# The peak of gate times up from magnitudes in one VectorE pass, and signed products made by batch in the down stage

## The chip, the cores and the metric

The kernel runs on one core of a Trainium2 chip. The metric is the device time of one execution in microseconds (us). PE is TensorE (its weight loads are PEld), DVE is VectorE, ACT is ScalarE, POOL is GpSimd, and SP is the engine whose queue issues most transfers.

## What is computed

`x` is 32 sequences of 128 tokens with 256 features. Four layers are added to it in turn: a cross-attention by correlation, a product in the frequency domain, a sampled cross-attention, and a feed-forward block whose tensors are all rounded to whole multiples of a unit. The change touches only the last:

```python
def act_qdq(x):
    qmax = 2.0 ** (ACT_BITS - 1) - 1.0        # ACT_BITS = 16
    scale = jnp.maximum(jnp.max(jnp.abs(x)) / qmax, 1e-12)
    return jnp.clip(jnp.round(x / scale), -qmax - 1.0, qmax) * scale
x = act_qdq(x)
up = act_qdq(x @ lpbq_dequant(w_up).T)
gate = act_qdq(x @ lpbq_dequant(w_gate).T)
sig = fixed_qdq_u16(jax.nn.sigmoid(gate))
gate = act_qdq(gate * sig)
o = act_qdq(gate * up)
return o @ lpbq_dequant(w_down).T
```

Each `act_qdq` divides by a unit that comes from the largest magnitude of the whole tensor, so nothing can be rounded before all of the tensor has been seen. `gate` and `up` have 768 features for each of the 4096 tokens.

## The kernel before

The program is written engine by engine, each with its own list of instructions, and every order and wait (semaphores) is set by hand. The features of the feed-forward block lie over the 128 partitions in IC = 6 groups, the tokens along the free dimension. Three sizes of work occur: a quad (4 sequences, 512 tokens, 8 of them), a half (256 tokens, 128x1536 elements with the six groups, HALVES = 16 of them), and a sequence (128 tokens, 128x768 elements, B = 32).

The gated product lies in `wide` (float, all tokens). `up` doesn't fit beside it: PE makes it in the stage before, ACT copies it out (`keep_up`, L1037), DVE takes its peak (`peak_up`, L1997), and the SP queue stores it to `up_far` in device memory (L593) and brings it back quad by quad into three places `ups` (L598 and L607). `up_slot` says which place a quad uses. From the fourth quad on, a transfer waits for `up_whole`, that is until ACT has read the quad that was there.

Peak stage, by halves. ACT divides `up` by its unit and writes int16 (`whole_up`, L1081, tile `upq`), and the same for the gated values (`whole_g2`, L1087, tile `g2q`), four buffers each, so that half h waits for `o_done` of half h-4 (h-3 products done). DVE multiplies the two (`hidden_product`, L2114) and writes the float product back into `wide`, then reduces it to the largest magnitude (`peak_product`, L2119), one half behind. `make_unit(4, ...)` (L1999 to L2028) turns the 16 maxima into a unit: one reduction, a transpose on PE (`spread_peak`, L1524), a second reduction and five steps on one column. PE waits for `o_peak` of 14 halves and then has three long matmuls without use (`keep_wide`, L1584) ahead of the transpose, and three behind it; they are two instructions each.

Down stage, by sequences. `staggered(engine, B, steps)` issues, at tick t, each step for sequence t minus its lag, in the order of the list. ACT multiplies the product by the inverse unit and adds a large constant, which rounds it (`round_o`, L1102); DVE subtracts the constant (`whole_hidden`, L2133); PE multiplies by the weights, 12 instructions for a sequence (`down_product`, L1591), into one of two banks; DVE scales the result and adds it to `x_sb` (`add_y`, L2138, lag 2). The SP queue stores two sequences at a time (L611), each store behind its wait for `y_done`.

Memory is laid out by hand: names that are opened and closed at once (`scrap`, `sq`, `upq` and so on) lie over others that are not alive at the same time.

Of the kernel before, what the change touches and what calls it, by code (L numbers as in the profile page):

```python
# [18 lines left out]
F32 = mybir.dt.float32  # L19
# [178 lines left out]
def build(nc, x, ctx_in, wq, wk, wv, wo, bq, bk, bv, bo, wfr, wfi, bf, wval, bval, woff, boff,  # L198
# [7 lines left out]
    with ExitStack() as ctx:  # L206
        def sem(name):
            return ctx.enter_context(nc.semaphore(name))

        def sb(name, shape, dt=F32, scope=ctx):  # L210
            return scope.enter_context(nc.sbuf_tensor(name, shape, dt))
# [19 lines left out]
        mid = sb("mid", [128, 6, 128])  # L231
        SAME, CROSS, MA, MB, INV, MEAN = (mid[:, i, :] for i in range(6))
        xn = sb("xn", [128, 4, D])
        tr_sb = sb("tr_sb", [128, 2, DC, 128])
# [173 lines left out]
            sem("gate_whole"), sem("sig_done"), [sem(f"sig_whole_{e}") for e in ("dve", "pool")], sem("g2_done"))  # L408
        up_whole, g2_whole, o_done, o_peak = sem("up_whole"), sem("g2_whole"), sem("o_done"), sem("o_peak")
        o_round, o_whole, down_out, y_done = sem("o_round"), sem("o_whole"), sem("down_out"), sem("y_done")  # L410
# [26 lines left out]
        def gate_half(h):  # L437

            return wide[:, :, h * 256:(h + 1) * 256]
# [19 lines left out]
        def up_slot(t):  # L459

            return (1, 0, 2)[t % 3]


        def ccx_rows(g):
# [60 lines left out]
        def _(sp):  # L525
# [74 lines left out]
            for t in range(1, NQ):  # L600
                for j in range(3):
                    sp.wait_ge(up_stored[j], 16 * (NQ if t == 2 else t + 1))
                if t == 2:
                    sp.wait_ge(up_peak, UPS)
                if t >= 3:
                    sp.wait_ge(up_whole, 2 * (t - 2))
                sp.dma_start(ups[:, up_slot(t)], up_far[:, t]).then_inc(up_back[t % 3], 16)  # L607
            sp.wait_ge(x3_done, 2 * NQ)
            for i in range(B // 2):
                sp.wait_ge(y_done, (i + 1) * 2)  # L610
                sp.dma_start(outr[:, i * 2:(i + 1) * 2, :], x_sb[:, i * 2:(i + 1) * 2, :]).then_inc(stored, 16)  # L611
# [158 lines left out]
        def _(act):  # L770
# [303 lines left out]
            def whole_up(h):  # L1074

                t = h // 2
                if h % 2 == 0:
                    act.wait_ge(up_back[t % 3], 16 * (t // 3 + 1))
                if h >= 4:
                    act.wait_ge(o_done, h - 3)  # L1080
                nc.scalar.activation(upq[:, h % 4], ups[:, up_slot(t), :, h % 2 * 256:(h % 2 + 1) * 256], ACT.Copy, scale=unit[:, 2, 3:4]).then_inc(up_whole, 1)  # L1081

            def whole_g2(h):

                if h >= 4:
                    act.wait_ge(o_done, h - 3)
                nc.scalar.activation(g2q[:, h % 4], gate_half(h), ACT.Copy, scale=unit[:, 3, 3:4]).then_inc(g2_whole, 1)  # L1087

# [9 lines left out]

            def round_o(b, s):
                if late(b, 2):  # L1100
                    act.wait_ge(o_whole, b - 1)
                nc.scalar.activation(hid[:, 2 + s], wide[:, :, at_seq(b)], ACT.Identity, scale=unit[:, 4, 3:4], bias=unit[:, 7, 0:1]).then_inc(o_round, 1)  # L1102

            act.wait_ge(unit_step, 1 + 5 * 5)
            staggered(act, B, [(0, round_o)])

        @block.tensor
        def _(pe):
# [477 lines left out]
            def down_product(b, s):  # L1586
                pe.wait_ge(o_whole, b + 1)
                if late(b, 2):
                    pe.wait_ge(y_done, b - 1)
                for ic in range(IC):  # L1590
                    last = mm(bank[s][:, 0:D], hid[:, s, ic, :], wdT[:, ic, :], start=(ic == 0), stop=(ic == IC - 1))  # L1591
                last.then_inc(down_out, 1)

            pe.wait_ge(up_kept, UPS)
            pe.wait_ge(o_peak, HALVES - 2)
            keep_wide(3)
# [5 lines left out]
        def _(dve):  # L1602
# [506 lines left out]

            def hidden_product(h):  # L2110

                dve.wait_ge(up_whole, h + 1)
                dve.wait_ge(g2_whole, h + 1)
                V.tensor_tensor(gate_half(h), upq[:, h % 4], g2q[:, h % 4], ALU.mult).then_inc(o_done, 1)  # L2114

            def peak_product(h):

                dve.wait_ge(o_done, h + 1)
                V.tensor_reduce(peak[:, 4, h:h + 1], gate_half(h), AX.XY, ALU.max, apply_absolute_value=True).then_inc(o_peak, 1)  # L2119

            for h in range(HALVES + 1):
                if h < HALVES:
                    hidden_product(h)
                if h:
                    peak_product(h - 1)
            dve.wait_ge(o_peak, HALVES)
            make_unit(4, HALVES)

            def whole_hidden(b, s):
                dve.wait_ge(o_round, b + 1)  # L2130
                if late(b, 2):
                    dve.wait_ge(down_out, b - 1)
                V.tensor_scalar(hid[:, s], hid[:, 2 + s], MAGIC, None, ALU.subtract).then_inc(o_whole, 1)  # L2133

# [4 lines left out]

            staggered(dve, B, [(0, whole_hidden), (2, add_y)])  # L2140

# [20 lines left out]
```

## Time and profile before

| what | value |
|---|---|
| runs of this kernel | 866.13, 871.84, 871.96 us, median 871.84 |
| the profiled execution | 868.69 us |
| its span in the profile | 866.2 us |
| mean granted clock of PE | 0.941 of full speed |
| busy, of the span | PE 84%, DVE 74%, ACT 54%, POOL 29% |

The span runs from the first to the last instruction of the profiled execution. Times in a trace are from the span's start. A pass is shown with its own duration; on ACT and DVE the next one may start before the last has ended, so start-to-start times are a little shorter than durations.

### The profile page before, as it was taken

What the parts mean: (1) busy time and instruction counts of PE and PEld (TensorE: products, weight loads), DVE (VectorE), ACT (ScalarE), POOL (GpSimd) and SP (SyncE); (2) the same over time, 40 slices, a digit from 0 to 9 for tenths busy, and PEclk for the clock granted to TensorE, in tenths of its full rate; (3) what the DMA queues carried; (4) which work ended last, traced back from release to release, by engine and by line L of the source; (5) the groups of instructions that cost most, each with busy time, mean ns of one, the idle gap of its engine ahead of it and who ended that gap; (6) DMA issues with size and microseconds to landing.
All of it is one profiled execution on the core that took longest, in us unless ns stands there. A gap on an engine that the chain in (4) does not pass through costs nothing.

```text
span 866.2 us, 10711 instructions
## 1 busy us (share of the span) xinstructions
PE 727.4 (84%) x3599; PEld 485.6 (56%) x3599; DVE 639.0 (74%) x1184; ACT 465.5 (54%) x818; POOL 249.8 (29%) x198
## 2 busy tenths in 40 slices
PE   4999998799977788767999987999979990039998
PEld 4878886578766567523455553444434440018887
DVE  3577799966798579955999975877569997993333
ACT  2444455455334668855655512344379959934441
POOL 3000000576784112365676720000023320000000
PEclk9999999799999999889999997999999995559999
DMA  8900000050143300000000000000014339501111
GB/s 279 349 12 1 1 1 0 1 135 1 30 139 85 35 1 1 2 1 1 2 2 1 1 2 0 1 0 1 0 73 163 158 147 403 219 0 37 49 52 58
DMA packets 32122, 52.87 MB, mean 61 GB/s; under 512 B 3523, under 2 KB 27331, under 8 KB 30918
## 3 DMA queue, kind: packets, MB, share of 16 engines
q1 hardware_dynamic: 30256, 50.62, 17.7%
q10 hardware_dynamic: 1814, 1.59, 0.6%
q8 instruction: 29, 0.48, 0.2%
q14 instruction: 23, 0.19, 0.1%
HBM read 35.34 MB, written 16.84 MB: 60 GB/s over the span
## 4 chain that ended last, share of the span: by engine, by line
PE 41%; ACT 11%; DVE 8%; issue 4%; DMA 1%; POOL 0%; SPq 0%; DVEq 0%; ACTq 0%; POOLq 0%
PE pair L1544 10%; PE pair L1591 10%; PE pair L1472 4%; PE pair L1440 4%; PE pair L1455 3%; DVE wide L2085 3%; PE pair L1483 2%; ACT upq L1081 2%; ACT g2q L1087 2%; PE pair L1332 2%; PE pair L1335 2%; ACT wide L1050 1%; DVE peak L1997 1%; PE pair L1569 1%; DMA ups<-up_far 1%
## 5 line engine op out<-in xcount | busy, mean ns | idle before, releaser
L1932 DVE SCALAR_TENSOR_TENSOR hat<-pair,hat 128x1024 f32<-128x1024 f32 x64 | 78.0, 1218 | 29.5 <-ACT hat L970 18.2
L970 ACT ACTIVATE hat<-pair 128x1024 f32<-128x1024 f32 x64 | 65.5, 1024 | 60.9 <-PE pair L1440 60.9
L1569 PE MATMUL pair<-xqs,wuT 128*128 128x512 f32 x192 | 84.6, 601 | 4.7 <-ACT up_stage L1037 4.7
L1544 PE MATMUL pair<-xqs,wgT 128*128 128x512 f32 x192 | 85.4, 603 | 0.0
L1591 PE MATMUL pair<-wdT,hid 128*128 128x256 f32 x384 | 83.1, 379 | 0.4 <-DVE hid L2133 0.4
L723 POOL TENSOR_TENSOR hat<-hat 128x1024 f32<-128x1024 f32 x30 | 70.7, 2357 | 41.3 <-DVE hat L1932 41.3
L1591 PEld LDWEIGHTS pair<-wdT,hid 128*128 128x128 f32 x384 | 72.9, 190 | 11.1 <-DVE hid L2133 1.2
L1569 PEld LDWEIGHTS pair<-xqs,wuT 128*128 128x128 f32 x192 | 36.8, 194 | 51.3 <-issue 51.1
L1152 PE MATMUL pair<-wT,ft_sb 128*128 128x256 f32 x256 | 63.8, 392 | 0.0
L623 POOL TENSOR_TENSOR rstd<-lnt,half 128x8 f32<-128x8 f32 (+2 forms) x15 | 26.4, 1760 | 129.5 <-DVE lnt L1635 129.5
L1102 ACT ACTIVATE hid<-wide,unit 128x768 f32<-128x768 f32 x32 | 32.5, 1026 | 57.2 <-DVE hid L2133 43.7
L1544 PEld LDWEIGHTS pair<-xqs,wgT 128*128 128x128 f32 x192 | 36.8, 195 | 43.7 <-issue 43.7
L1018 ACT ACTIVATE wide<-pair 128x512 f32<-128x512 f32 x48 | 28.7, 597 | 57.1 <-PE pair L1544 57.1
L2133 DVE TENSOR_SCALAR hid<-hid 128x768 f32<-128x768 f32 x32 | 17.9, 560 | 51.1 <-PE pair L1591 49.6
L1606 DVE BATCH_NORM_STATS2 stats<-x_sb 128x6 f32<-128x256 f32 x128 | 50.8, 414 | 5.3 <-DMA x_sb<-in_x_dram 5.3
L1152 PEld LDWEIGHTS pair<-wT,ft_sb 128*128 128x128 f32 x256 | 46.0, 189 | 12.2 <-issue 7.3
L749 POOL CAST xqs<-xqT 128x1024 f32<-128x1024 int16 x16 | 19.2, 1198 | 116.2 <-ACT xqT L1011 77.9
L1584 PE MATMUL pair<-wdT 128*128 128x512 f32 x12 | 7.7, 794 | 52.9 <-DVE peak L2119 52.9
L796 ACT ACTIVATE qq<-pair 128x256 f32<-128x256 f32 x32 | 12.3, 383 | 65.8 <-PE pair L1155 65.8
L1650 DVE TENSOR_SCALAR xn<-x_sb,rstd,nmr 128x256 f32<-128x256 f32 x96 | 46.4, 483 | 1.4 <-PE pair L1315 1.1
L1292 PE MATMUL pair<-fold,tr_sb 128*128 128x256 f32 x128 | 35.2, 399 | 12.7 <-DVE x_sb L1785 10.3
L1725 DVE TENSOR_TENSOR ab<-qq,pair 128x512 f32<-128x512 f32 x32 | 21.9, 686 | 30.1 <-ACT qq L798 29.8
(243 smaller groups left out, 1711.8 us busy)
## 6 DMA issues: line engine op xcount, KB each, us to landing
up_far<-up_stage SPq DMA_DIRECT2D x24, 512.0 KB, 2.6
ups<-up_far SPq DMA_DIRECT2D x8, 1536.0 KB, 6.9
x_sb<-in_x_dram SPq DMA_DIRECT2D x8, 512.0 KB, 7.4
c_sb<-in_ctx_dram SPq DMA_DIRECT2D x8, 512.0 KB, 8.7
ctx<-in_ctx_dram SPq DMA_DIRECT2D x32, 128.0 KB
out_dram<-x_sb SPq DMA_DIRECT2D x16, 256.0 KB, 2.1
ctx<-in_ctx_dram SPq DMA_DIRECT2D x16, 126.0 KB
four<-in_c_four_dram SPq DMA_DIRECT2D x1, 1280.0 KB, 6.6
```

The costliest lines, as they stand in the source:

```text
L723: nc.gpsimd.tensor_tensor(ramp(4 * u + 2), ramp(4 * u), ramp(4 * u + 2), ALU.add).then_inc(summed, 1)
L970: nc.scalar.activation(ramp(n), sides_of(n)[:].rearrange("p i t -> p (i t)"), ACT.Relu).then_inc(relu_done, 1)
L1152: mm(bank[2 + s][:, i * D:(i + 1) * D], ft_sb[:, s, i * DC + c, :], wT[:, i, c, :], start=False, stop=(i == 1 and c == DC - 1))
L1292: last = mm(bank[6 + s][:, 0:D], tr_sb[:, s, c, :], fold[:, c, :], start=(c == 0), stop=(c == DC - 1))
L1440: last = mm(sides_of(n)[:, i, :], sel[half, n % NP, :], rows[half, q, c * 2 + a, :], start=True, stop=True)
L1472: last = mm(bank[5][:, b * D:(b + 1) * D], attT[:, q % 2, c, (2 * i + b) * L:(2 * i + b + 1) * L], wout_sb[:, c, :], start=False, stop=(c ...
L1544: last = mm(bank[2 + oc][:], wgT[:, c, oc * 128:(oc + 1) * 128], xqs[:, s, c, :], start=(c == 0), stop=(c == DC - 1))
L1569: last = mm(bank[2 + oc], wuT[:, c, oc * 128:(oc + 1) * 128], xqs[:, t % 2, c, :], start=(c == 0), stop=(c == DC - 1))
L1591: last = mm(bank[s][:, 0:D], hid[:, s, ic, :], wdT[:, ic, :], start=(ic == 0), stop=(ic == IC - 1))
L1606: V.bn_stats(stats[:, at(b), :].rearrange("p o s -> p (o s)"), x_sb[:, at(b), :].rearrange("p o d -> p (o d)")).then_inc(bn_done[n], 1)
L1650: V.tensor_scalar(xn[:, b % 4, :], x_sb[:, at(b), :].rearrange("p o d -> p (o d)"), rstd[:, at(b)], nmr[:, at(b)], ALU.mult, ALU.add).then ...
L1932: V.scalar_tensor_tensor(ramp(n), sides_of(n)[:].rearrange("p i t -> p (i t)"), 0.0, ramp(n), ALU.max, ALU.add).then_inc(hat_done, 1)
```

## The change

ACT makes magnitudes (Abs) for the peak stage in place of signed whole parts. DVE multiplies two of them and keeps the largest in one pass (`tensor_tensor_reduce`); the product itself goes to a tile `scrap` that nobody reads, so `wide` keeps the gated values. In the down stage the signed parts are made again for one sequence at a time: the gated part on DVE (`signed_gate`), the up part on ACT (`signed_up`), their product times the inverse unit on DVE into int16 (`whole_product`), and its float form on ACT (`widen_o`) into four buffers `hid` in place of two. For this the SP queue reads `up_far` a second time (`up_again`), into two of the three places. Two of these eight transfers stand ahead of the output stores, the others between them. `add_y` moves from lag 2 to lag 3.

```diff
--- before.py
+++ after.py
@@ -230,6 +230,9 @@
         attT_place.close()
         mid = sb("mid", [128, 6, 128])
         SAME, CROSS, MA, MB, INV, MEAN = (mid[:, i, :] for i in range(6))
+        scrap_place = ExitStack()
+        scrap = sb("scrap", [128, IC, 256], F32, scrap_place)
+        scrap_place.close()
         xn = sb("xn", [128, 4, D])
         tr_sb = sb("tr_sb", [128, 2, DC, 128])
         peak = sb("peak", [128, 5, 64])
@@ -406,7 +409,7 @@
         up_stored, up_back = [sem(f"up_stored{i}") for i in range(3)], [sem(f"up_back{i}") for i in range(3)]
         gate_whole, sig_done, sig_whole, g2_done = (
             sem("gate_whole"), sem("sig_done"), [sem(f"sig_whole_{e}") for e in ("dve", "pool")], sem("g2_done"))
-        up_whole, g2_whole, o_done, o_peak = sem("up_whole"), sem("g2_whole"), sem("o_done"), sem("o_peak")
+        up_whole, g2_whole, o_done = sem("up_whole"), sem("g2_whole"), sem("o_done")
         o_round, o_whole, down_out, y_done = sem("o_round"), sem("o_whole"), sem("down_out"), sem("y_done")
         xn3_ready, tr3_done, tr3_copied = sem("xn3_ready"), sem("tr3_done"), sem("tr3_copied")
         mm3_done, v_kept, off_kept = sem("mm3_done"), sem("v_kept"), sem("off_kept")
@@ -460,6 +463,10 @@
 
             return (1, 0, 2)[t % 3]
 
+
+        def again_slot(r):
+
+            return 2 - r % 2 * 2
 
         def ccx_rows(g):
 
@@ -605,8 +612,18 @@
                 if t >= 3:
                     sp.wait_ge(up_whole, 2 * (t - 2))
                 sp.dma_start(ups[:, up_slot(t)], up_far[:, t]).then_inc(up_back[t % 3], 16)
+
+            def up_again(r):
+
+                sp.wait_ge(up_whole, HALVES + (r - 1) * QUAD if r >= 2 else HALVES - 4 + 4 * r)
+                sp.dma_start(ups[:, again_slot(r)], up_far[:, r]).then_inc(up_back[2 - r % 2], 16)
+
+            up_again(0)
+            up_again(1)
             sp.wait_ge(x3_done, 2 * NQ)
             for i in range(B // 2):
+                if i % 2 == 0 and i // 2 + 2 < NQ:
+                    up_again(i // 2 + 2)
                 sp.wait_ge(y_done, (i + 1) * 2)
                 sp.dma_start(outr[:, i * 2:(i + 1) * 2, :], x_sb[:, i * 2:(i + 1) * 2, :]).then_inc(stored, 16)
             sp.wait_ge(stored, 16 * (B // 2))
@@ -1078,13 +1095,13 @@
                     act.wait_ge(up_back[t % 3], 16 * (t // 3 + 1))
                 if h >= 4:
                     act.wait_ge(o_done, h - 3)
-                nc.scalar.activation(upq[:, h % 4], ups[:, up_slot(t), :, h % 2 * 256:(h % 2 + 1) * 256], ACT.Copy, scale=unit[:, 2, 3:4]).then_inc(up_whole, 1)
+                nc.scalar.activation(upq[:, h % 4], ups[:, up_slot(t), :, h % 2 * 256:(h % 2 + 1) * 256], ACT.Abs, scale=unit[:, 2, 3:4]).then_inc(up_whole, 1)
 
             def whole_g2(h):
 
                 if h >= 4:
                     act.wait_ge(o_done, h - 3)
-                nc.scalar.activation(g2q[:, h % 4], gate_half(h), ACT.Copy, scale=unit[:, 3, 3:4]).then_inc(g2_whole, 1)
+                nc.scalar.activation(g2q[:, h % 4], gate_half(h), ACT.Abs, scale=unit[:, 3, 3:4]).then_inc(g2_whole, 1)
 
             act.wait_ge(unit_step, 1 + 3 * 5)
             act.wait_ge(xqs_ready, 2 * NQ)
@@ -1096,13 +1113,25 @@
                 if h + 2 < HALVES:
                     whole_g2(h + 2)
 
-            def round_o(b, s):
-                if late(b, 2):
-                    act.wait_ge(o_whole, b - 1)
-                nc.scalar.activation(hid[:, 2 + s], wide[:, :, at_seq(b)], ACT.Identity, scale=unit[:, 4, 3:4], bias=unit[:, 7, 0:1]).then_inc(o_round, 1)
-
-            act.wait_ge(unit_step, 1 + 5 * 5)
-            staggered(act, B, [(0, round_o)])
+            def signed_up(b, s):
+
+                r = b // QUAD
+                if b % QUAD == 0:
+                    act.wait_ge(up_back[2 - r % 2], 16 * (r // 2 + 3 + r % 2))
+                if late(b, 2):
+                    act.wait_ge(o_round, b - 1)
+                else:
+                    act.wait_ge(o_done, HALVES - 3 + b)
+                nc.scalar.activation(upq[:, s, :, 0:128], ups[:, again_slot(r), :, b % QUAD * 128:(b % QUAD + 1) * 128], ACT.Copy,
+                                     scale=unit[:, 2, 3:4]).then_inc(up_whole, 1)
+
+            def widen_o(b, s):
+                act.wait_ge(o_round, b + 1)
+                if late(b, 4):
+                    act.wait_ge(down_out, b - 3)
+                nc.scalar.activation(hid[:, b % 4], g2q[:, 2 + s, :, 0:128], ACT.Copy).then_inc(o_whole, 1)
+
+            staggered(act, B, [(0, signed_up), (1, widen_o)])
 
         @block.tensor
         def _(pe):
@@ -1588,11 +1617,11 @@
                 if late(b, 2):
                     pe.wait_ge(y_done, b - 1)
                 for ic in range(IC):
-                    last = mm(bank[s][:, 0:D], hid[:, s, ic, :], wdT[:, ic, :], start=(ic == 0), stop=(ic == IC - 1))
+                    last = mm(bank[s][:, 0:D], hid[:, b % 4, ic, :], wdT[:, ic, :], start=(ic == 0), stop=(ic == IC - 1))
                 last.then_inc(down_out, 1)
 
             pe.wait_ge(up_kept, UPS)
-            pe.wait_ge(o_peak, HALVES - 2)
+            pe.wait_ge(o_done, HALVES - 2)
             keep_wide(3)
             spread_peak(4)
             keep_wide(3)
@@ -2107,37 +2136,41 @@
             dve.wait_ge(up_peak, UPS)
             make_unit(2, UPS)
 
-            def hidden_product(h):
+            def peak_product(h):
 
                 dve.wait_ge(up_whole, h + 1)
                 dve.wait_ge(g2_whole, h + 1)
-                V.tensor_tensor(gate_half(h), upq[:, h % 4], g2q[:, h % 4], ALU.mult).then_inc(o_done, 1)
-
-            def peak_product(h):
-
-                dve.wait_ge(o_done, h + 1)
-                V.tensor_reduce(peak[:, 4, h:h + 1], gate_half(h), AX.XY, ALU.max, apply_absolute_value=True).then_inc(o_peak, 1)
-
-            for h in range(HALVES + 1):
-                if h < HALVES:
-                    hidden_product(h)
                 if h:
-                    peak_product(h - 1)
-            dve.wait_ge(o_peak, HALVES)
+                    dve.wait_ge(o_done, h)
+                V.tensor_tensor_reduce(scrap[:], upq[:, h % 4], g2q[:, h % 4], 1.0, 0.0, ALU.mult, ALU.max,
+                                       accum_out=peak[:, 4, h:h + 1]).then_inc(o_done, 1)
+
+            def signed_gate(b, s):
+                if late(b, 2):
+                    dve.wait_ge(o_round, b - 1)
+                else:
+                    dve.wait_ge(o_done, HALVES - 3 + b)
+                V.tensor_scalar(g2q[:, s, :, 0:128], wide[:, :, at_seq(b)], unit[:, 3, 3:4], None, ALU.mult).then_inc(g2_whole, 1)
+
+            for h in range(HALVES):
+                peak_product(h)
+            dve.wait_ge(o_done, HALVES)
             make_unit(4, HALVES)
 
-            def whole_hidden(b, s):
-                dve.wait_ge(o_round, b + 1)
-                if late(b, 2):
-                    dve.wait_ge(down_out, b - 1)
-                V.tensor_scalar(hid[:, s], hid[:, 2 + s], MAGIC, None, ALU.subtract).then_inc(o_whole, 1)
+            def whole_product(b, s):
+                dve.wait_ge(g2_whole, HALVES + b + 1)
+                dve.wait_ge(up_whole, HALVES + b + 1)
+                if late(b, 2):
+                    dve.wait_ge(o_whole, b - 1)
+                V.scalar_tensor_tensor(g2q[:, 2 + s, :, 0:128], upq[:, s, :, 0:128], unit[:, 4, 3:4], g2q[:, s, :, 0:128],
+                                       ALU.mult, ALU.mult).then_inc(o_round, 1)
 
             def add_y(b, s):
                 dve.wait_ge(down_out, b + 1)
                 xb = x_sb[:, at(b), :].rearrange("p o d -> p (o d)")
                 V.scalar_tensor_tensor(xb, bank[s][:, 0:D], unit[:, 4, 2:3], xb, ALU.mult, ALU.add).then_inc(y_done, 1)
 
-            staggered(dve, B, [(0, whole_hidden), (2, add_y)])
+            staggered(dve, B, [(0, signed_gate), (1, whole_product), (3, add_y)])
 
 
 _INS = ["x", "ctx_1024", "L0_xattn_Wq", "L0_xattn_Wk", "L0_xattn_Wv", "L0_xattn_Wo", "L0_xattn_bq", "L0_xattn_bk",
```

## Rows read from the trace of the kernel before

**Rows 1.** The page: busy tenths in 40 slices of the span; PEclk is the granted clock.
```profile
PE   4999998799977788767999987999979990039998
DVE  3577799966798579955999975877569997993333
ACT  2444455455334668855655512344379959934441
PEclk9999999799999999889999997999999995559999
```

**Rows 2.** Windows: busy us and (count) of each engine, granted clock, DMA share, GB/s.
```profile
740.00:760.00 20.00, 0.00 (x0) 0.00 (x0) 20.00 (x13) 20.00 (x14) 0.00 (x0) 0.50 0.54 204
...
716.00:718.00 2.00, 0.00 (x0) 0.00 (x0) 1.28 (x2) 2.00 (x3) 0.00 (x0) 0.98 0.83 219
...
774.00:776.00 2.00, 2.00 (x4) 0.67 (x2) 2.00 (x2) 0.00 (x0) 0.00 (x0) 0.51 0.00 0
776.00:778.00 2.00, 1.88 (x6) 0.74 (x5) 1.41 (x7) 0.00 (x0) 0.00 (x0) 1.00 0.00 0
```

**Rows 3.** Groups after 600 us: busy us, mean ns, idle before in us, releaser.
```profile
L1591 PE MATMUL pair<-wdT,hid 128*128 128x256 f32 x384 | 83.1, 379 | 0.4 <-DVE hid L2133 0.4
...
L2085 DVE CUSTOM_DVE_ANT_0 wide<-sq,gq 128x1536 f32<-128x1536 uint16 x16 | 34.2, 2142 | 0.0
L1102 ACT ACTIVATE hid<-wide,unit 128x768 f32<-128x768 f32 x32 | 32.5, 1026 | 57.2 <-DVE hid L2133 43.7 <-DVE unit L2027 13.5
...
L2114 DVE TENSOR_TENSOR wide<-upq,g2q 128x1536 f32<-128x1536 int16 x16 | 28.0, 1749 | 3.1 <-issue 1.7 <-ACT upq L1081 1.4
L2119 DVE TENSOR_REDUCE peak<-wide 128x1 f32<-128x1536 f32 x16 | 27.8, 1743 | 0.0
L1050 ACT ACTIVATE wide<-gq,unit 128x1536 f32<-128x1536 int16 x16 | 25.0, 1565 | 0.0
...
L1081 ACT ACTIVATE upq<-ups,unit 128x1536 int16<-128x1536 f32 x16 | 24.9, 1563 | 1.0 <-DMA ups<-up_far 0.6 <-DVE unit L2025 0.4
...
L2133 DVE TENSOR_SCALAR hid<-hid 128x768 f32<-128x768 f32 x32 | 17.9, 560 | 51.1 <-PE pair L1591 49.6 <-ACT hid L1102 1.5
...
L2138 DVE SCALAR_TENSOR_TENSOR x_sb<-pair,unit,x_sb 128x256 f32<-128x256 f32 x32 | 15.3, 478 | 3.7 <-PE pair L1591 3.7
...
L2080 DVE TENSOR_SCALAR sq<-wide 128x1536 uint16<-128x1536 f32 x12 | 11.4, 952 | 0.0
```

**Rows 4.** The chain that ended last, from 761 us: start, us, what.
```profile
761.77 2.94 ACT upq L1081 x2
...
773.11 3.33 DVE peak L2119 x2
776.47 0.18 DVE unit L2002
...
779.97 83.16 PE pair L1591 x384
```

**Rows 5.** Line L2085 alone (ns min/median/max) and its reads on DVE.
```profile
L2085 DVE CUSTOM_DVE_ANT_0 wide<-sq,gq x16: 1744/1751/3921, 644.7 to 709.7; 128x1536 f32<-128x1536 uint16 x16
...
709.68 0.07 DVE L2085 DVE_READ_ACCUMULATOR2_ANT peak<- 128x1 f32 x1
```

**Rows 6.** PE's timeline around the peak's transpose: start, us.
```profile
771.59 4.99 PE L1584 MATMUL pair<-wdT 128*128 128x512 f32 x6 [52.94 <-DVE peak L2119]
...
776.85 2.74 PE L1584 MATMUL pair<-wdT 128*128 128x512 f32 x6
```

**Rows 7.** Lines alone, ns min/median/max: no scalar, one scalar from memory, two sources.
```profile
L1842 DVE TENSOR_SCALAR tx<-off x8: 280/281/694, 302.7 to 365.4; 128x256 f32<-128x256 f32 x8
...
L2043 DVE TENSOR_SCALAR xn<-xn,unit x32: 344/349/1159, 523.4 to 603.0; 128x256 f32<-128x256 f32 x32
...
L1863 DVE SCALAR_TENSOR_TENSOR ccx<-tx,ccx x8: 424/425/426, 308.3 to 372.6; 128x256 f32<-128x256 f32 x8
```

**Rows 8.** DMA issues after 700 us: KB each, median us from issue to landing.
```profile
ups<-up_far SPq DMA_DIRECT2D x8, 1536.0 KB, 6.9
```

## The prediction

> **What bounds the kernel now.** I read four views, from coarse to fine. The page's slices come first [rows 1]: the change touches the last seven of them or so (one slice is 21.7 us). There PE is empty for two slices while DVE is full and ACT nearly so, then PE is full for four slices while DVE and ACT stand at 3 to 4 tenths. So two stages with different limits follow each other: a peak stage (what is the largest |gate times up|?) and a down stage (the last matrix product). The windows say the same in numbers: between 740 and 760 us DVE and ACT are both busy for all 20.00 us [rows 2].
>
> The groups then show what fills the peak stage [rows 3]. ACT makes 32 passes of 1.56 us (L1081 and L1087; back to back they start 1.47 us apart, 2.94 us for two in rows 4), with 1.0 us of idle time in all before them. DVE makes 16 products (L2114, 1.75 us) and 16 reductions (L2119, 1.74 us), also touching (3.33 us for two in rows 4), with 3.1 us idle. Per half, ACT needs 2.94 us and DVE 3.33 us, so DVE ends last.
>
> The chain shows by how much [rows 4]: ACT's last pass ends at 761.77 + 2.94 = 764.71; DVE still has three products and four reductions and ends them at 776.47, 11.76 us later. The unit (reduction, transpose on PE, six small DVE steps) takes to 778.2, the first rounding on ACT and DVE to 779.97, and then PE does 384 matmuls in 83.16 us without a break: 2.60 us for each of 32 sequences. The end is set by PE from there, and the way to 779.97 by DVE.
>
> **The peak stage, part by part.** Removed: 16 products and 16 reductions, 16 x 3.33 = 53 us of DVE. Added: 16 fused passes. The trace has the same operation in the gate stage (L2085: two 16-bit integer sources, 1536 elements, a maximum kept): 1.744 us at best, 1.751 in the middle, with 0.07 us for reading the maximum behind it [rows 5]; from one start to the next that is 1.67, as for the two reductions of rows 4, plus the read. Its longest is 3.92 us; its group mean is 2.14 [rows 3]. I take 1.75 + 0.07, since GpSimd has no work in this stage, and keep 2.14 as the upper end: two passes stand on the path, so 0.8 us.
>
> ACT's passes keep their number and size; only Copy becomes Abs. No row shows Abs. The nearest, Copy (1.56) and Sigmoid on the same shape (1.565, L1050 [rows 3]), agree, so I take no difference. The bounds: nothing, or 32 x 0.01 = 0.3 us. ACT waited for DVE nowhere, so it ends where it ended, at 764.71, and is now the bound.
>
> DVE is no longer two reductions behind. The pass for half 14 can start at 763.2 and is done, with its read, at 765.0; each pass waits for the one before, so that for half 15 ends at 766.8, and the peak's reduction starts at 766.9 in place of 776.47: 9.6 us earlier. What is late next is PE. Its three long matmuls before the transpose wait for half 13, whose last ACT pass ends 4 x 1.47 us before 764.7, at about 760.3, plus 1.8 us: 762.1. They took 4.99 us [rows 6] and are in front of the transpose in PE's queue; they end at 767.2, 0.1 us after the transpose could start. Saving at the unit: 9.45 us.
>
> **From the unit to the first matmul.** Before: one ACT pass (1.04), one DVE pass (0.57) and hand-overs, 1.8 us. Now, all after the unit in DVE's order: signed gate 0, signed gate 1, product 0, then the widening on ACT. The signed up parts 0 and 1 are no burden: they wait for halves 12 and 13 only, and ACT is free from 764.7.
> Signed gate, 768 elements, float to int16 with one scale from memory. L2133 has the shape without such a scale, 0.56 us [rows 3]; one such scale costs 344 - 281 = 63 ns on the 256-element forms [rows 7]. I take 0.62, 0.54 from start to start; the ends are 0.56 and 1.0 (a reduction's speed).
> Product, 768 elements, int16 in and out, one scale from memory. Between L1863 (256 elements, 425 ns [rows 7]) and L2114 (1536, 1749 ns) an element costs 1.034 ns, so 768 cost 0.955 us, and 1.02 with the scale. The lower end is half the elements' time, 0.62; the upper end a pass of double length, 1.75.
> Widening on ACT, int16 to float: between half of 1.56 (0.78) and 1.03 (L1102, the same size with scale and bias from memory [rows 3]); I take 0.9.
> Sum: 2 x 0.54 + 1.02 + 0.9 + 0.1 for hand-overs = 3.1 us, against 1.8: 1.3 us given back. Saving 9.45 - 1.3 = 8.15 us.
>
> **The down stage.** Per sequence ACT now has two passes (signed up 0.9, widening 0.9) where it had one of 1.03: 1.8 us. DVE has 0.62 + 1.02 + 0.48 (L2138) = 2.1 us where it had 1.04. PE has 2.60 us. Both are covered, DVE by 0.5 us. The order holds too: when product b-3 leaves PE, DVE adds it, makes gate b+1 and product b and is done 2.1 us later, ACT widens to 3.0 us, and PE wants it at 5.2 us. Output sums now come third in DVE's tick, but each still waits for PE.
> The up parts are read again: eight transfers of 1536 KB, 6.9 us each in the middle [rows 8], two before the stage and six in it. In the SP queue each stands in front of a pair of output stores. Transfer r is issued when signed part 4r-5 is made, about when PE starts sequence 4r-8, and its data are first needed at sequence 4r-3: 4 x 2.60 us or more for 6.9, and two further periods before PE would notice. A blocked store delays nothing that is waited for, since nothing reuses x_sb. Cost 0; a transfer would need some 17 us to cost anything. The last sum, store and end stay as they are.
>
> **A rule against the change.** The product is the operation scalar_tensor_tensor with two SBUF sources that are no bf16. L1863 has two such float sources and took 425 ns for 256 elements, L2085 and L2114 two int16-sized sources at 1.04 ns an element [rows 3, 7]. The Trainium skill (Vector Engine (DVE) Microarchitecture Reference, "Points that are easy to get wrong") says that this shape with two non-bf16 SBUF sources runs at half throughput. By that rule the product would take the upper end above; the rows speak against it, but none has this operation on int16. The rival below prices it from rows.
>
> **Sum.** The profiled execution took 868.69 us (span 866.2). 868.69 - 8.15 = 860.5. The three other runs are 866.13, 871.84 and 871.96; the middle of all four is 870.3, 1.6 above the profiled one. I forecast 870.3 - 8.15, about 862 us. That is 0.94% less, just under the 1% that a measurement of this kernel can tell from no change.
>
> **Rivals.**
> A. The clock. PE starts its filler at 1.2 GHz and was granted 2.4 GHz some 4.3 us later [rows 2, 6]; the second filler took 2.74 us and the down product followed 0.4 us after it. Now the second filler ends near 770.0 and the down product starts near 771.8. For it: a longer gap, and another moment of the rise. Against: in 714 to 718 the clock stayed at 0.98 to 1.00 with PE idle for over 2 us [rows 2]. If the down product starts at 1.2 GHz for 4.3 us it loses 2.2 us, and a slow second filler 0.5: saving 5.5, 865 us.
> B. DVE becomes the bound of the down stage because the product runs at half speed: 0.48 + 0.62 + 1.75, less two overlaps of 0.08, is 2.7 us per sequence, 0.1 x 31 = 3 us more, and 0.7 at the start: 866.
> C. The other side: both the product and the gate pass run at their upper ends, 0.48 + 1.0 + 1.75 - 0.16 = 3.07 us per sequence. That is 0.47 x 31 = 14.6 us, and 1.5 at the start: 870.3 - 8.15 + 16.1 = 878 us. It is slower than before from 2.60 + 8.15 / 31 = 2.86 us per sequence on. For it: neither operation is in the trace on int16. Against: L2133 and L2080 (0.95 us for 1536) show the float-to-integer pass at double speed [rows 3].
> D. The reload is late after all (a transfer of over 17 us in a stage with stores): each microsecond costs up to six. Nothing in rows 8 is near it; 868 for a transfer of 18 us.
> E. The product runs at its lower end, for which only the skill has a reason (VectorE: DVE Perf Modes, the perf-mode table: two-source operations on 16-bit data reach double speed; no row here has 16-bit output): 0.4 us better, 861.5.
>
> **Chances.** Forecast with E 0.70 (own range 859 to 865, most of it the spread of runs), A 0.14, B 0.05, C 0.05, D 0.03, other 0.03. The range from 857 to 868.5 takes in A, B and D and leaves out C. Faster by over 1% needs a saving of 8.7 us: within the forecast's bounds and the runs' spread about 4 in 7, so 0.40; within 1%: the rest of the forecast, A, B and D, 0.52; slower 0.08.
>
> **What would show it.** Right: ACT passes 1.56 us in an unbroken row ending near 764.7; fused passes of 1.75 with idle time before each on ACT; the unit's reduction near 766.9; first down matmul near 771.8 and 83.2 us of unbroken matmuls. Wrong: PE idle before L1591's groups released by ACT's widening or DVE; a granted clock under 1.00 after 772; a product over 1.1 us; ACT waiting for a DMA of up_far; a transfer beyond 10 us.

## The result, and the profile after

The changed kernel took 861.13 us (median of 857.53, 859.42, 862.84 and 863.90); the kernel before took 870.46 us (the three runs in the table before the change and one of 869.08). The ratio is 0.9896, with an interval from 0.9859 to 0.9934: 1.0% faster, 9 us, with an uncertainty of 3 us. The forecast was about 862 us. Two further comparisons gave 0.9905 (0.9869 to 0.9941) and 0.9877 (0.9839 to 0.9915). All three agree with the 0.94% of the prediction and none can say on which side of 1% the change lies.

The chain of the changed kernel, from ACT's last passes on (start, us, what), answers to [rows 4]:

```profile
764.51 1.48 ACT upq L1098
...
766.01 1.76 DVE scrap L2145
...
767.95 1.76 DVE scrap L2145
...
769.76 0.18 DVE unit L2031
...
772.66 0.94 DVE g2q L2165
...
773.62 0.85 ACT hid L1132
...
774.51 83.16 PE pair L1620 x384
```

Read it backwards. The down matmuls last 83.16 us, as before to the last digit. In front of them stand the widening (ACT), the first product and, between 771.5 and 772.66, two gate passes; then the unit. ACT's last pass ended at 767.45, as its timeline says (the last two passes as one row):

```profile
764.42 3.03 ACT L1098 ACTIVATE upq<-ups,unit 128x1536 int16<-128x1536 f32 x2
```

From there to the unit DVE now has the rest of one fused pass and one whole one, where it had seven passes: 2.3 us (767.45 to 769.76) in place of 11.8.

The groups after 712 us (busy us, mean ns | idle before, releaser), against [rows 3]:

```profile
L1620 PE MATMUL pair<-wdT,hid 128*128 128x256 f32 x384 | 83.1, 379 | 1.6 <-ACT hid L1132 1.6
...
L2165 DVE SCALAR_TENSOR_TENSOR g2q<-upq,unit,g2q 128x768 int16<-128x768 int16 x32 | 32.4, 1012 | 0.0
L1125 ACT ACTIVATE upq<-ups,unit 128x768 int16<-128x768 f32 x32 | 29.3, 919 | 0.0
L2145 DVE CUSTOM_DVE_ANT_0 scrap<-upq,g2q 128x1536 f32<-128x1536 int16 x16 | 28.1, 1759 | 18.7 <-ACT upq L1098 16.8 <-issue 1.7 <-DVE peak L2145 0.2
L1132 ACT ACTIVATE hid<-g2q 128x768 f32<-128x768 int16 x32 | 27.0, 843 | 31.5 <-DVE g2q L2165 31.5
L1098 ACT ACTIVATE upq<-ups,unit 128x1536 int16<-128x1536 f32 x16 | 24.9, 1561 | 0.8 <-DMA ups<-up_far 0.5 <-DVE unit L2054 0.4
L1104 ACT ACTIVATE g2q<-wide,unit 128x1536 int16<-128x1536 f32 x16 | 24.9, 1560 | 0.0
L2153 DVE TENSOR_SCALAR g2q<-wide,unit 128x768 int16<-128x768 f32 x32 | 19.5, 611 | 0.1
L2171 DVE SCALAR_TENSOR_TENSOR x_sb<-pair,unit,x_sb 128x256 f32<-128x256 f32 x32 | 15.5, 484 | 24.3 <-PE pair L1620 24.3
```

The idle column is where to read the bound. In the peak stage it is now DVE that waits for ACT: L2145 waited 16.8 us for ACT's up part (L2114 of the kernel before: 1.4), while ACT's passes have 0.8 us in all (before: 1.0). In the down stage DVE's idle time stands before L2171, which waits for PE, and PE waited once, 1.6 us at the start.

The same stretches in every run, each from the timelines of one profiled execution, in us. "ACT" is from the start of the first gated pass to the end of the last up pass; "peak" from there to the unit's reduction; "unit" to its last copy; "start" to the first down matmul; "down" all 384 matmuls; "sum" from the first gated pass to the end of the last output sum.

| run | ACT | peak | unit | start | down | sum |
|---|---|---|---|---|---|---|
| before | 48.22 | 11.77 | 1.71 | 1.79 | 83.15 | 147.15 |
| after | 48.06 | 2.31 | 1.72 | 3.03 | 83.15 | 138.79 |
| a0_after | 48.20 | 2.32 | 1.71 | 3.04 | 83.15 | 138.94 |
| a1_after_again | 48.22 | 2.31 | 1.72 | 3.04 | 83.15 | 138.95 |
| e1_fused_signed | 48.31 | 2.31 | 1.89 | 1.78 | 83.15 | 137.95 |
| e2_gate_early | 48.31 | 2.31 | 1.88 | 1.98 | 83.15 | 138.15 |
| e3_no_reload | 48.16 | 2.30 | 1.96 | 3.04 | 83.15 | 139.13 |
| e4_gate_twice | 48.23 | 2.30 | 1.87 | 4.10 | 84.83 | 141.85 |
| e8_gates_long_filler | 48.32 | 2.31 | 1.89 | 4.09 | 83.15 | 140.28 |
| e5_product_twice | 48.36 | 2.31 | 1.88 | 3.97 | 88.68 | 145.72 |
| e9_products_long_filler | 48.24 | 2.31 | 1.72 | 3.97 | 88.29 | 145.04 |
| e6_no_filler | 48.44 | 2.31 | 1.71 | 3.05 | 85.24 | 141.27 |
| e7_shared | 43.57 | 2.50 | 2.08 | 1.99 | 83.15 | 133.81 |
| e10_shared_again | 43.84 | 2.50 | 1.92 | 1.98 | 83.15 | 133.91 |

The last column repeats to 0.2 us for the same kernel, where whole times spread over 6 to 8 us; so most of what follows is read from it.

### The profile page after: what moved, and what is told of

Its sections match the earlier page's. It is cut to its first block, busy times and chain, and to the rows that moved or that the text cites. A ratio compares the mean times of both kernels' runs of the same rounds, so it can differ in the third digit from the quotient of the medians.

```text
span 862.1 us, 10821 instructions
## 1 busy us (share of the span) xinstructions
PE 730.6 (85%) x3599; PEld 486.7 (56%) x3599; DVE 644.9 (75%) x1216; ACT 486.4 (56%) x850; POOL 250.1 (29%) x198
## 4 chain that ended last, share of the span: by engine, by line
PE 41%; ACT 11%; DVE 8%; issue 4%; DMA 1%; POOL 0%; SPq 0%; DVEq 0%; ACTq 0%; POOLq 0%
PE pair L1573 10%; PE pair L1620 10%; PE pair L1501 4%; PE pair L1469 4%; PE pair L1484 4%; DVE wide L2114 3%; ACT g2q L1104 2%; PE pair L1512 2%; PE pair L1361 2%; PE pair L1364 2%; ACT wide L1067 1%; DVE peak L2026 1%; ACT upq L1098 1%; PE pair L1598 1%; DMA ups<-up_far 1%
## 5 line engine op out<-in xcount | busy, mean ns | idle before, releaser
L1132 ACT ACTIVATE hid<-g2q 128x768 f32<-128x768 int16 x32 | 27.0, 843 | 31.5 <-DVE g2q L2165 31.5
L1469 PE MATMUL pair<-rows,sel 64*128 64x512 bf16 x256 | 44.0, 402 | 0.8 <-ACT off L898 0.8
L1814 DVE TENSOR_TENSOR x_sb<-pair,x_sb 128x256 f32<-128x256 f32 x64 | 26.7, 417 | 23.2 <-PE pair L1257 17.4
```

The costliest lines, as they stand in the source:

```text
L1469: last = mm(sides_of(n)[:, i, :], sel[half, n % NP, :], rows[half, q, c * 2 + a, :], start=True, stop=True)
```

## The experiments

**Is it the change at all, and is the rest chance?** The first profile after differed in two more places: it came to the peak stage 2.9 us later than the profile before, and needed 3.93 us from the last sum to the end (the tail), in place of 2.58. Runs a0 and a1 are the changed kernel unaltered.

> The changed kernel itself once more, beside the three that follow. Theory 1 (the steps of the prediction): from the last up part of ACT in the peak stage to the first down matmul 7.1 us (15.3 before), 83.2 us of down matmuls in one row; 8.2 us less than before. Theory 2 (the 2.7 us that the first profile lost before the peak stage and the 1.3 us after its last sum belong to the change): they stand in this profile too. If they are chance they do not come back together.

> The changed kernel once more: 139 us from ACT's first gated pass to the last sum, 0.99 of the kernel before; the span before that pass varies with the clock granted between 360 and 420 us, and longer where it is lower.

Measured: 860.33 and 858.54 us, 8.2 us less than before in the last column. The first gated pass started at 715.53 and 713.94 us (before 716.48, first profile after 719.39), and the tail was 3.78 and 2.58. The tail was also 4.08 us in e1, which reads up_far once only, and 2.57 to 2.58 in all the others. Theory 2 falls: a1 has neither, and e1 has the long tail without the new down stage. What makes a tail long stays open. a1, whose granted clock between 360 and 420 us was 0.89, came to the peak stage first of all, as expected; but the kernel before came 2.5 us later at the same 0.89, so the stages ahead of 360 us move it too.

**The fused pass alone.** e1 keeps the old down stage and leaves out the negative side of the peak.

```diff
-                V.tensor_tensor(gate_half(h), upq[:, h % 4], g2q[:, h % 4], ALU.mult).then_inc(o_done, 1)
...
-                V.tensor_reduce(peak[:, 4, h:h + 1], gate_half(h), AX.XY, ALU.max, apply_absolute_value=True).then_inc(o_peak, 1)
...
+                V.tensor_tensor_reduce(gate_half(h), upq[:, h % 4], g2q[:, h % 4], 1.0, 0.0, ALU.mult, ALU.max,
+                                       accum_out=peak[:, 4, h:h + 1]).then_inc(o_done, 1)
```

> The kernel before with the fused pass alone: signed parts, the product still written into wide, the largest product kept in the same pass; down stage as before. It leaves out the negative side of the peak (the fused pass knows no magnitude), so its unit can be too small. Theory 1: the unit's reduction starts 9.6 us earlier than before, the first down matmul 1.8 us after the unit, 9.4 us less than before and 1.2 less than the changed kernel. If writing the product into wide in place of the scrap tile costs something, the pass is longer than 1.76 us.

Measured: 861.57 us, ratio 0.9888 (0.9843 to 0.9934); 9.2 us less in the last column than before, 1.0 less than the changed kernel. The pass writes its product into wide here and not into scrap, and took as long, 1.76 us:

```profile
740.75 1.76 DVE L2116 CUSTOM_DVE_ANT_0 wide<-upq,g2q 128x1536 f32<-128x1536 int16 x1 [1.17 <-ACT upq L1081]
```

All of the gain is the fused pass, and the whole price of the rebuilt down stage is its start, 1.78 against 3.04 us.

**The price of the start.** e2 makes one gate pass in DVE's idle time of the peak stage and the next behind the product.

```diff
             for h in range(HALVES):
+                if h == HALVES - 2:
+                    signed_gate(0, 0)
                 peak_product(h)
...
-            staggered(dve, B, [(0, signed_gate), (1, whole_product), (3, add_y)])
+            staggered(dve, B, [(1, whole_product), (0, later_gate), (3, add_y)])
```

(later_gate is signed_gate for all sequences but the first.)

> The first signed gate part moves ahead of the fused pass for half 14, where DVE is idle for 1.17 us, and in the down stage the product is issued ahead of the next gate part. If two gate passes of 0.54 us from start to start stand on the path to the first down matmul, it starts 1.07 us earlier after the unit (1.95 us from the end of the unit in place of 3.0), and the time falls by 1.1 us (0.13%). If the clock is what sets the start, or ACT's widening is held by something else, nothing changes.

Measured: start 1.98 us, 1.06 less, as expected; 859.54 us, ratio 0.9884 (0.9855 to 0.9913). A gain of 0.8 us in the last column (the unit took 0.17 longer in this profile) can't be told from nothing in whole times; the timeline tells it.

**The second reading of up_far.** e3 drops the calls of up_again and the waits for them.

> Leaves out the second reading of up_far: no transfers, no waits for them; the signed up parts of the down stage are made from what lies in the two places. Theory 1 (the eight transfers are hidden): same time as the changed kernel within 0.3%, first down matmul and its 83.2 us unchanged. Rival D (transfers cost something, in a wait or as traffic beside PE, or in the tail behind the last stores): the down stage or the time from the last sum to the end gets shorter, by 1.3 us if the tail is due to them.

Measured: 861.22 us, ratio 0.991 (0.9877 to 0.9942), 139.13 us in the last column against 138.94. In the changed kernel the six transfers that fell in the down stage took 6.5 us in the middle, and none of the eight took over 7.1:

```profile
ups<-up_far SPq DMA_DIRECT2D x6, 1536.0 KB, 6.5
out_dram<-x_sb SPq DMA_DIRECT2D x16, 256.0 KB, 2.4
```

The stores' median landing was 2.1 us without them and 2.4 with. Nobody waits for a store but the end. Rival D is excluded: 12.6 MB are read again at no cost in time.

**How much cover does DVE have in the down stage?** e4 makes every gate pass twice, e5 every product, the copy going to free room.

```diff
+                V.scalar_tensor_tensor(upq[:, 2 + s, :, 0:128], upq[:, s, :, 0:128], unit[:, 4, 3:4], g2q[:, s, :, 0:128],
+                                       ALU.mult, ALU.mult)
                 V.scalar_tensor_tensor(g2q[:, 2 + s, :, 0:128], upq[:, s, :, 0:128], unit[:, 4, 3:4], g2q[:, s, :, 0:128],
                                        ALU.mult, ALU.mult).then_inc(o_round, 1)
```

> The changed kernel with every signed gate pass made twice (the other copy into free room). Per sequence DVE then has 1.94 + 0.54 = 2.48 us of 2.60. Theory 1 (DVE is covered by PE up to 2.60 us per sequence): only the first two gate passes cost, 1.1 us; the down matmuls stay at 83.2 us. If the cover is smaller than the idle time says, PE shows gaps before its groups.

> The changed kernel with every product of the down stage made twice: 1.94 + 0.93 = 2.87 us of DVE per sequence, as if the product ran at half speed. Theory 1: DVE sets the pace, the down stage grows by 31 x 0.27 = 8.4 us and 0.9 at the start, 9.3 in all, which gives back all of the gain. If PE falls to its lower clock in the gaps of 0.27 us, it grows by tens of us. If the cover is larger than thought, less than 5 us.

Measured: e4 864.74 us (0.9932, 0.9906 to 0.9958), e5 867.27 (0.996, 0.994 to 0.9981). In the last column e4 costs 2.9 us where 1.1 was expected, e5 6.8 where 9.3 was. Neither fits. (In whole times e5 is 3.5 us under the kernel before, in the last column 1.4; as this stretch repeats to 0.2 us, I go by it.) DVE's timeline in e5 shows one half of it, three sums in turn:

```profile
789.18 0.48 DVE L2173 SCALAR_TENSOR_TENSOR x_sb<-pair,unit,x_sb 128x256 f32<-128x256 f32 x1
...
791.96 0.48 DVE L2173 SCALAR_TENSOR_TENSOR x_sb<-pair,unit,x_sb 128x256 f32<-128x256 f32 x1
...
794.74 0.48 DVE L2173 SCALAR_TENSOR_TENSOR x_sb<-pair,unit,x_sb 128x256 f32<-128x256 f32 x1
```

They stand 2.78 us apart with no idle time, not 2.87. In the changed kernel DVE's idle time before this instruction is 0.65 us of 2.59:

```profile
785.18 0.48 DVE L2171 SCALAR_TENSOR_TENSOR x_sb<-pair,unit,x_sb 128x256 f32<-128x256 f32 x1 [0.65 <-PE pair L1620]
785.58 0.61 DVE L2153 TENSOR_SCALAR g2q<-wide,unit 128x768 int16<-128x768 f32 x1
786.11 1.01 DVE L2165 SCALAR_TENSOR_TENSOR g2q<-upq,unit,g2q 128x768 int16<-128x768 int16 x1
787.77 0.48 DVE L2171 SCALAR_TENSOR_TENSOR x_sb<-pair,unit,x_sb 128x256 f32<-128x256 f32 x1 [0.65 <-PE pair L1620]
```

The sum starts 0.65 us after the product's end (787.12). Once it no longer waits it starts 0.08 us before that end (in e5, 788.25 + 1.01 is 789.26 and the sum starts at 789.18). So the cover is 0.65 + 0.08 us; 0.93 more makes 2.59 + 0.93 - 0.73 = 2.79, and 2.78 was measured. This fits. What is left is e4's down stage, 84.83 us.

**The clock.** e6 takes away the three long matmuls behind the transpose (one line, keep_wide(3)), so that PE idles longer before the down stage.

> The changed kernel without the three long matmuls behind the transpose: PE then stands idle for 4.2 us from the transpose to the first down matmul, in place of 1.6. Rival A in its strong form (a longer gap costs the clock): the granted clock falls to 0.50 and the first 4.3 us or so of down matmuls run at 1.2 GHz, 2.2 us more. If the gap does not matter: no change, the down matmuls stay at 83.2 us.

Measured: down 85.24 us, 862.18 us in all (0.9908, 0.9876 to 0.994). The windows of e6 (busy us and counts of PE, PEld, DVE, ACT, POOL, granted clock, DMA):

```profile
770.00:772.00 2.00, 0.93 (x3) 0.13 (x1) 1.48 (x6) 0.14 (x1) 0.00 (x0) 1.00 0.89 362
772.00:774.00 2.00, 0.00 (x0) 0.00 (x0) 1.90 (x7) 0.00 (x0) 0.00 (x0) 0.75 0.77 326
774.00:776.00 2.00, 0.45 (x1) 0.45 (x2) 1.97 (x3) 1.35 (x2) 0.00 (x0) 0.50 0.00 0
776.00:778.00 2.00, 2.00 (x6) 1.56 (x6) 1.75 (x3) 2.00 (x4) 0.00 (x0) 0.50 0.03 8
778.00:780.00 2.00, 2.00 (x7) 1.62 (x6) 0.00 (x0) 1.49 (x2) 0.00 (x0) 0.54 0.56 111
780.00:782.00 2.00, 2.00 (x11) 1.77 (x10) 1.46 (x3) 0.00 (x0) 0.00 (x0) 1.00 0.97 412
```

The clock was at 2.4 GHz, fell to 1.2 in a gap of 4.21 us, and PE made 6 or 7 matmuls in 2 us in place of 11 until about 780: 2.09 us lost. The mean of 0.75 in 772 to 774, between 1.00 and 0.50, puts the fall at about 773.0, and PE's last instruction before it had ended at 771.33:

```profile
771.01 0.32 PE L1553 MATMUL pair<-big,unit 128*128 128x128 f32 x1 [0.41 <-DVE unit L2030]
775.55 85.24 PE L1620 MATMUL pair<-wdT,hid 128*128 128x256 f32 x384 [4.21 <-ACT hid L1132]
```

e4 has a gap too, and its clock fell (windows as above):

```profile
770.00:772.00 2.00, 0.00 (x0) 0.00 (x0) 1.97 (x4) 0.59 (x1) 0.00 (x0) 1.00 0.00 0
772.00:774.00 2.00, 1.69 (x7) 1.47 (x8) 1.97 (x4) 1.56 (x3) 0.00 (x0) 0.88 0.04 8
774.00:776.00 2.00, 2.00 (x6) 1.55 (x5) 1.60 (x3) 1.56 (x3) 0.00 (x0) 0.50 0.00 0
```


```profile
766.87 2.74 PE L1613 MATMUL pair<-wdT 128*128 128x512 f32 x6
772.31 84.83 PE L1620 MATMUL pair<-wdT,hid 128*128 128x256 f32 x384 [2.69 <-ACT hid L1132]
```

Its clock was at 2.4 GHz all through the gap and fell at about 773.5, 1.2 us after PE had begun again. The changed kernel's gap is shorter, and its clock stayed at 1.00 through it and behind it:

```profile
770.14 2.74 PE L1613 MATMUL pair<-wdT 128*128 128x512 f32 x6
774.51 20.77 PE L1620 MATMUL pair<-wdT,hid 128*128 128x256 f32 x95 [1.63 <-ACT hid L1132]
```

To tell the gap from the third DVE pass, e8 and e9 are e4 and e5 with keep_wide(5) in place of keep_wide(3) behind the transpose.

> As the one with every gate pass made twice, where the down matmuls took 84.83 us in place of 83.15 after a gap of 2.69 us, but with five long matmuls behind the transpose in place of three, so that the gap is about 0.9 us. If the fall of the granted clock after the gap made the 1.7 us, they go: 83.15 us. If DVE's third pass in the first ticks made them, 84.8 us stay.

> As the one with every product made twice (88.68 us of down matmuls, gap 2.56 us), with five long matmuls behind the transpose, gap about 0.7 us. It separates the two costs: if the clock's fall and DVE's pace add up, about 87 us; if the slow matmuls at the start only hid a part of DVE's excess (0.18 us per sequence), between 87 and 88.7.

Measured: e8 864.65 us, its down stage back at 83.15:

```profile
771.06 4.46 PE L1613 MATMUL pair<-wdT 128*128 128x512 f32 x10
776.49 83.15 PE L1620 MATMUL pair<-wdT,hid 128*128 128x256 f32 x384 [0.97 <-ACT hid L1132]
```

DVE's work is that of e4, so all 1.68 us of e4 were the clock after the gap, and DVE at 2.48 us of 2.60 costs PE nothing. (Each of e4, e5, e6, e8 and e9 has one profile; how often the clock falls after such a gap is not shown.) e9: 865.02 us, down 88.29 with the clock at 1.00 from its start on. DVE's pace alone therefore makes 5.14 of e5's 5.53 us (0.18 for each of some 29 sequences), and the fall of the clock only 0.39 there: the likely reason, argued and not shown by itself, is that slow matmuls at the start stand where PE would have waited for DVE later. The two delays don't add up.

**A version that beats both.** With DVE idle 16.8 us of the peak stage and ACT full, e7 moves the gated parts of halves 4, 8 and 12 to DVE, on top of e2. These halves are made signed, so they get a second fused pass with factor -1 for the negative side, which gives the same peak.

```diff
+                V.tensor_scalar(g2q[:, h % 4], gate_half(h), unit[:, 3, 3:4], None, ALU.mult).then_inc(g2_dve, 1)
...
+                if h in G2_DVE:
+                    j = G2_DVE.index(h)
+                    dve.wait_ge(g2_dve, 2 * j + 1)
+                    V.tensor_tensor_reduce(scrap[:], upq[:, h % 4], g2q[:, h % 4], -1.0, 0.0, ALU.mult, ALU.max,
+                                           accum_out=peak[:, 4, HALVES + j:HALVES + j + 1]).then_inc(g2_dve, 1)
```

> As the one with the early gate part, and the gated parts of halves 4, 8 and 12 are made by DVE, signed, with a second fused pass of factor -1 for the negative side (3 x (1.0 + 1.83) us more on DVE, 3 x 1.47 us less on ACT). Theory 1 (ACT bounds the peak stage, DVE idles 1.17 us per half): ACT ends 4.4 us earlier, in all 5.4 us less than the changed kernel. Theory 3 (DVE or the transfers of up_far bound the stage as well): a wait of ACT for a transfer or for o_done takes the place, and under 2 us are gained.

> The version with three gated halves on DVE and the early gate part once more, beside the changed kernel, since its first median lay 2.5 us under the changed kernel's and its trace 5.1 us. If the trace is right and the difference is the spread of the stages before, the two comparisons together give 4 to 6 us less than the changed kernel.

Measured: 857.88 and 858.32 us, ratios 0.9876 (0.9842 to 0.9911) and 0.9858 (0.9825 to 0.989). In the last column 133.81 and 133.91 us, 5.1 less than the changed kernel in both profiles. ACT's passes, 13 in place of 16, still have no gap:

```profile
L1104 ACT ACTIVATE upq<-ups,unit 128x1536 int16<-128x1536 f32 x16 | 24.6, 1560 | 0.8 <-DMA ups<-up_far 0.4 <-DVE unit L2060 0.3
L1110 ACT ACTIVATE g2q<-wide,unit 128x1536 int16<-128x1536 f32 x13 | 20.2, 1559 | 0.0
```

Theory 1 holds in the trace: ACT bounded the stage, and no transfer took its place (0.4 us of waiting). In whole times the gain is smaller: the mean of 12 runs is 857.9 us against 860.3 for 12 runs of the changed kernel in the same two comparisons, 2.5 us less with an interval from 0.2 to 4.7. That the trace's 5.1 us lie just outside stays open; the spread of the stages before the peak stage, below, is of that size.

## Why the prediction was right

- **The bound.** ACT ends where it did and DVE no longer behind it: predicted 2.2 us from ACT's end to the unit's reduction, measured 2.31; a fused pass was 1.76 with 0.08 for the read, predicted 1.75 and 0.07. Abs costs what Copy costs (1.561 and 1.560 against 1.563 and 1.560 us). The saving to that point, 9.6 us predicted, is 11.77 - 2.31 = 9.46. (The prediction writes 4 x 1.47 us for the passes behind ACT's part of half 13; they are three, and 3 x 1.47 gives the 760.3 that it goes on with.)
- **PE ahead of the transpose.** Predicted as 0.1 us late. In the changed kernel PE was in time, since the clock rose a little earlier in the first filler (4.74 us in place of 4.99); in others the filler took up to 5.45 us and the unit 1.87 to 1.96 us. So the term was 0 or up to 0.3 us from one profile to the next, with the moment at which the clock rose.
- **The start.** Predicted 3.1 us in place of 1.8, measured 3.03 in place of 1.79. Its parts: gate pass 0.61 (0.62 predicted), product 1.01 (1.02), widening 0.84 (0.9). e2 shows the two gate passes to stand on the path.
- **The down stage.** 83.15 us before and after. DVE works 1.94 us of 2.59 per sequence (predicted 2.1 and an idle time of 0.5; durations were added without the 0.08 us by which neighbours overlap). e4 with e8 shows that even 2.48 us are covered, e3 that the transfers are.
- **The sum.** Predicted 8.15 us, measured 8.2 to 8.4 in the last column, 9 with 3 of uncertainty in whole times. That it fits to 0.1 us is in part luck: the stretch to the unit was 0.1 us over its size, and PE's lateness of 0.1 us didn't come.
- **The rule against the change.** The product on int16 took 1.012 us for 768 elements; less the 0.063 us for a scale from memory that is 0.949, and up to the 1.749 us for 1536 elements of L2114 each element costs 1.04 ns, the slope of the rows before. The rule of the Trainium skill (Vector Engine (DVE) Microarchitecture Reference, "Points that are easy to get wrong") would have made it 1.75: the measurement decides against it here. The double speed that rival E took from the Trainium skill (VectorE: DVE Perf Modes, the perf-mode table) did not come either: that table names tensor_tensor, and this operation stayed at 1.04 ns an element. (That no row has 16-bit output is so for two-source passes; L2080 in [rows 3] has one source and writes uint16.)
- **Rivals.** A was priced right and didn't happen: e6 lost 2.09 us where 2.2 were predicted. But it was nearer than its chance of 0.14 may suggest: a gap of 1.63 us kept the clock, 2.56 to 2.69 us lost it. The row that the prediction held against A shows less than it seems to: the 0.98 of 716 to 718 is already a fall, at about 717.9, some 2.4 us after the matmuls of the up stage had ended at 715.53. The clock held for 2.4 us there, and only for some 1.7 in e6.

```profile
711.93 3.60 PE L1569 MATMUL pair<-xqs,wuT 128*128 128x512 f32 x8
...
718.00:720.00 2.00, 0.47 (x1) 0.18 (x1) 1.12 (x7) 1.65 (x3) 0.00 (x0) 0.50 0.99 406
```

- **B and C.** They needed a slower product or gate pass; neither happened. B's own sum, and C's with it, was off: without a wait all three of DVE's passes overlap by 0.08 us, so that B's 0.48 + 0.62 + 1.75 would be 2.61 us, hardly over PE's 2.59, and not 2.7. e5, with four passes (3.11 - 4 x 0.08 = 2.79, measured 2.78), bears out this way of counting.
- What was wrong is small: e5's expectation of 8.4 us (idle time read as the whole cover) and e4's, which left out the clock.

## What to carry to other kernels

When two engines share a stage, count each one's time per unit of work: taking 1.5 us per half from the slower gains only until the next one (here ACT, 0.4 us per half faster) sets the pace, and then work can be moved back. Cover behind a bound engine is worth using, but read it as idle time plus the overlap that returns when the wait goes, and check what the rebuilt start of the stage does to the gap in front of PE. Where whole times spread more than the effect, compare one stretch between two fixed instructions in each profile.

## What the runs showed of the hardware

- **The gap and the clock.** At the start of the down stage the granted clock stayed at 2.4 GHz through PE gaps of 0.85, 0.97 and 1.62 to 1.63 us (the last in four profiles), and fell to 1.2 GHz after gaps of 2.56 and 2.69 us and in one of 4.21 us, which cost up to 2.1 us of matmul time. A filler of two more long matmuls took the loss away. This is no safe limit: in e6 the fall came some 1.7 us after PE's last instruction, hardly longer than the gap that the changed kernel gets through, and in e4 and e5 it came 1.2 to 1.3 us after PE had begun again.
- **Where the spread of runs comes from.** In the sampled cross-attention, identical in all kernels here, the stretch from the start of ACT's first pass that writes hat (360 to 364 us) to the start of the last took between 140.5 and 147.0 us. From its end to the peak stage the profiles differ by 0.7 us at most. It follows the granted clock of the window from 360 to 420 us: 0.89 and 140.5 us before, 0.83 and 143.1 after, 0.80 and 144.3 in e3, 0.74 and 147.0 in e5; the other ten profiles keep the same order. The window of the kernel before and that of e5, with PE busy in part:

```profile
360.00:420.00 60.00, 42.46 (x317) 19.27 (x316) 38.65 (x48) 34.72 (x53) 33.45 (x21) 0.89 0.00 1
```

```profile
360.00:420.00 60.00, 45.18 (x285) 20.57 (x285) 32.33 (x36) 30.49 (x43) 31.93 (x20) 0.74 0.00 1
```

PE makes fewer matmuls in more busy time (285 in 45.18 us, 317 in 42.46). That this stage's short PE gaps let the clock fall at random is an inference from these rows; it was not tested by filling them.
